# The order of the last routing steps, and who loads the last batch's second-layer weights

## What is computed

```python
xn = _layernorm(x)
x = x + gnn(xn, src, dst, edge_weight) + mix(xn)     # message passing; linear attention over 8 heads, gelu
h = _layernorm(x)
probs = softmax(h @ gate_w + gate_b)                 # 8 experts, top 1
idx = argmax(probs)
pos = (cumsum(one_hot(idx), axis=0) * one_hot(idx)).sum(-1) - 1
kept = pos < C                                       # C = ceil(1.25 * 12500 / 8)
hmid = relu(buf[e] @ w1[e] + b1[e])                  # 256 -> 1024
y = hmid @ w2[e] + b2[e]                             # 1024 -> 256
x = x + nan_to_num(y[idx, pos] * prob * kept)
```

## Time and profile before

| | |
|---|---|
| median of 3 runs | 2496.98 us (2493.55 to 2497.48) |
| the profiled execution | 2497.35 us, of which the profile's span is 2495.6 us |
| TensorE | 2049.6 us busy (82%) |
| weight loads of TensorE | 1578.1 us (63%) |
| VectorE | 1511.6 us (61%) |
| ScalarE | 1033.6 us (41%) |
| GpSimd | 1849.9 us (74%) |
| DMA | 568.84 MB, 228 GB/s in the mean |

### The profile page before, as it was taken

How to read it: one execution, slowest core, us unless ns; L and a number is a source line. 1 busy time by engine, 2 the same in 40 slices (tenths; PEclk the granted TensorE clock), 3 DMA queues, 4 the chain that set the end, 5 groups by cost and what they waited for, 6 DMA issues and landing times. The chain is left out here.

```text
span 2495.6 us, 42607 instructions
## 1 busy us (share of the span) xinstructions
PE 2049.6 (82%) x12873; PEld 1578.1 (63%) x12873; DVE 1511.6 (61%) x5293; ACT 1033.6 (41%) x2479; POOL 1849.9 (74%) x1924
## 2 busy tenths in 40 slices
PE   0048999994677787998989989998989998787997
PEld 0015666662455565776768777776778777676986
DVE  6776555554358777787747556566565666565332
ACT  4663333331244444543434433443444444352332
POOL 7777777777777777777777777777777777765575
PEclk9999999996788887999999999999998999898999
DMA  9846666664566667777777777777887888778653
GB/s 337 321 138 178 174 175 175 175 172 128 150 195 201 194 190 255 237 238 222 244 232 227 248 231 234 233 229 253 304 295 273 306 304 293 249 274 305 239 180 108
DMA packets 279195, 568.84 MB, mean 228 GB/s; under 512 B 51493, under 2 KB 180142, under 8 KB 259791
## 3 DMA queue, kind: packets, MB, share of 16 engines
q0 software_dynamic: 98352, 268.90, 35.3%
q1 hardware_dynamic: 150225, 245.97, 28.9%
q10 hardware_dynamic: 30390, 51.21, 5.6%
HBM read 506.09 MB, written 87.86 MB: 238 GB/s over the span
## 5 line engine op out<-in xcount | busy, mean ns | idle before, releaser
L967 POOL DMA_INDIRECT rows_sb<-xn_scratch,src_sb x1517 | 1458.3, 961 | 462.2 <-issue 456.7
L1261 PE MATMUL bank<-acc 128*128 128x128 f32 (+1 forms) x2624 | 434.4, 319 | 3.6 <-ACT acc L2042 2.9
L1285 PE MATMUL bank<-acc 128*128 128x256 f32 x1680 | 413.1, 390 | 0.0
L1261 PEld LDWEIGHTS bank<-acc 128*128 128x128 f32 x2624 | 379.2, 202 | 27.3 <-issue 5.6
L1079 PE MATMUL bank<-rows_sb,s_sb 128*24 128x256 f32 x3082 | 229.7, 419 | 198.6 <-DMA rows_sb<-xn_scratch,src_sb 198.0
L2059 ACT ACTIVATE acc<-bank,acc 128x128 f32<-128x128 f32 (+1 forms) x656 | 211.9, 398 | 368.5 <-PE bank L1261 368.2
L1285 PEld LDWEIGHTS bank<-acc 128*128 128x128 f32 x1680 | 313.9, 194 | 48.8 <-issue 0.4
L1549 DVE TENSOR_TENSOR acc<-acc,bank 128x48 f32 x831 | 170.5, 205 | 264.8 <-PE bank L1089 150.2
L1079 PEld LDWEIGHTS bank<-rows_sb,s_sb 128*24 128x24 f32 x3082 | 85.5, 108 | 272.8 <-issue 240.4
L1976 ACT COPY sums<-bank 120x256 f32<-120x256 f32 x208 | 76.5, 368 | 355.6 <-PE bank L1079 355.5
L2007 ACT ACT_TABLE_LOAD x95 | 121.9, 1283 | 200.8 <-PE bank L1168 199.9
(11 more groups left out here) (277 smaller groups left out, 3633.7 us busy)
## 6 DMA issues: line engine op xcount, KB each, us to landing
acc<-ffn_first_in SPq DMA_DIRECT2D x64, 1028.0 KB
acc<-ffn_w_in SPq DMA_DIRECT2D x64, 1024.0 KB
arena<-xn_scratch SPq DMA_DIRECT2D x194, 128.0 KB, 3.1
h_scratch<-arena ACTq DMA_DIRECT2D x97, 256.0 KB
rows_sb<-xn_scratch,src_sb POOLq DMA_INDIRECT x1517
xnt_scratch<-arena SPq DMA_DIRECT2D x97, 128.0 KB, 2.3
arena<-xnt_scratch SPq DMA_DIRECT2D x97, 128.0 KB
arena<-x_in SPq DMA_DIRECT2D x97, 128.0 KB
```

The lines of the kernel that those rows point to most:

```text
L967: pool.indirect_dma_start(out=chunk_row(c), out_offset=None, in_=xn_d, in_offset=bass.IndirectOffsetOnAxis(ap=src_sb[:, c:c + 1], axis=0)) ...
L1261: m = pe.matmul(bank[:, i * tokens:(i + 1) * tokens], w1_sb[k % 2][:, h, f * P:(f + 1) * P], xt[:, k % 2, h, 0:tokens], start=h == 0, stop ...
L1285: m = pe.matmul(bank[:, i * D:(i + 1) * D], hid[:, f, i * P:(i + 1) * P], w2_sb[k % 2][:, f, :], start=False, stop=f == FC - 1 and i == 0)
```

## The change

Two edits, both for the last batch.

First, the order at places 215 to 220. On TensorE, tick 162, first(58, a), moves from ahead of "sums" to behind it. On VectorE, the spread for that tick stays ahead of the routing work (called by hand under "early"), the rank is read after the fourth of the seven tables, not after the seventh, and the two `finish_unit` steps of units 56 and 57 (places 215 and 216) move to the end of place 217, behind `fill_slots`. On GpSimd, the scatters of units 56 and 57 move from places 216 and 217 to place 218, behind the gathers of units 60 and 61. The wanted place of units of the last batch is one higher, so that the turn of unit 60 moves from place 219 (ahead, before first(59, b)) to place 220, behind second(59, a).

Second, the second-layer weights of units 64 to 81 are loaded by SyncE's `load_second`, for each of the 18 units, also where the expert is the one of unit k - 2. The 18 indirect DMAs of GpSimd fall away, the first-layer weights stay with GpSimd. The places (`w2_at`) stay: place 227 for unit 64, and every second one from there.

```diff
@@
-        new1_ld, new2_ld, rows_known = sems("new_w1_ld", 2), sems("new_w2_ld", 2), sem("rows_known")
+        new1_ld, rows_known = sems("new_w1_ld", 2), sem("rows_known")
@@
         sums_at = [p + 1 for p in chosen_at]
+        HELD = range(chosen_at[-1], last_c + 1)
+        assert HELD[0] > PAIRS and rank_at[-1] == sums_at[-1] == build_at[-1]
...
-        wanted_at = [slots_at[b] + (4 if slots_at[b] + 4 < PAIRS else 2) for b in batch_of]
+        wanted_at = [slots_at[b] + (4 if slots_at[b] + 4 < PAIRS else 2 if slots_at[b] < PAIRS else 3) for b in batch_of]
...
-            if e_place[n] == sums_at[-1] and ("unit", n - 1) not in here:
-                here.insert(0, ("unit", n))
-            elif e_place[n] >= PAIRS or ("unit", n - 1) in here or after == len(here):
+            if e_place[n] >= PAIRS or ("unit", n - 1) in here or after == len(here):
                 here.append(("unit", n))
...
-            asked = max(known - 1 + lag, turn_place[k] - ahead)
+            asked = max(known - 1 + lag if slots_at[batch_of[k]] < PAIRS else known, turn_place[k] - ahead)
...
-            scatter_at[min(done_place(k) + 1, PLACES - 1)].append(k)
+            scatter_at[last_c + 1 if done_place(k) in HELD else min(done_place(k) + 1, PLACES - 1)].append(k)
@@ sync_program
                 for k in w2_at[p]:
-                    if k not in SKIPS:
-                        load_second(k)
+                    load_second(k)
@@ gpsimd_program
-                for k in w2_at[p]:
-                    if k in SKIPS:
-                        load_new_second(k)
@@ tensor_program, second_layer
-                    if k in SKIPS:
-                        pe.wait_ge(new2_ld[k % 2], new_value(k))
-                    else:
-                        pe.wait_ge(w2_ld[k % 2], w2_value(k))
+                    pe.wait_ge(w2_ld[k % 2], w2_value(k))
@@ vector_program, side_step
                 elif kind == "early":
                     for t, s in c_steps(k, (2,)):
                         c_step(t, s)
+                    if k == sums_at[-1]:
+                        for n, at in enumerate(e_place):
+                            if at == k:
+                                unit_tick(n)
                     read_small(k, False)
                 elif kind == "end":
-                    read_small(k, True)
+                    if k != rank_at[-1]:
+                        read_small(k, True)
...
                         if build_at[t] == k:
                             build_table(t)
+                            if t == routes[-1][RT - 1]:
+                                read_small(k, True)
                 elif kind == "unit":
-                    unit_tick(k)
+                    if e_place[k] != sums_at[-1]:
+                        unit_tick(k)
@@ vector_program, the loop over places
-                for kind, k in side[p]:
-                    if kind == "unit" and p >= PAIRS:
-                        finish_unit(k)
+                if p >= PAIRS and p not in HELD or p == last_c:
+                    for n, at in enumerate(e_place):
+                        if at == p or p == last_c and at in HELD:
+                            finish_unit(n)
```

More of the change, by code:

```diff
@@ L1020, in load_new_first @@
                     bounds_check=NE * P - 1, oob_is_err=False).then_inc(new1_ld[k % 2], 16)
[L1022 to L1028, removed]
             for p in range(PLACES):
```

## The result

The changed kernel takes 2512.15 us (median of 6 runs, 2507.35 to 2519.01) against 2497.68 us of the kernel before (6 runs, 2493.55 to 2499.53): ratio 1.0055, 95% interval 1.0042 to 1.0067. It is 13.7 us slower by the ratio, where 3.8 us were forecast, and it lies outside the range.

What follows compares the result with a forecast made beforehand. In the last 230 us it saw the routing chain, token fetch and GpSimd's queue as bounds. Routing -2.0, GpSimd relieved -2.8, SyncE's queue +8.6 gave +3.8 us upon 2496.98: 2500.8 us, range 2492 to 2506.

Steps and rivals of the forecast that it cites:

- What bounds the kernel, and the mechanism: Last 230 us: routing chain and token fetch, GpSimd's 7.95 us a unit; then second-layer weights waiting behind load_back on SyncE.
- The forecast 2.8 us: Tail: GpSimd, relieved of 18 DMAs, no longer drops behind, so 2.3 and 0.53 us come back; lower bound 1.5.
- Landing behind load 7: Unit 67: second-layer weights land late behind load 7's megabyte on SyncE; wait taken as 3.0 us, bounds 0 to 4.5.
- rival (b): Units 67, 71: GpSimd's megabyte shares evenly, wait 4.5 us each; 2504.7 us, chance 0.30 with far parts of two other rivals.
- The clock: TensorE in the tail: a wait of 3 us costs about 1.1 us more afterwards at 1.2 GHz, range 0.9 to 1.6.
- Unit 75: Second layer of unit 75: half a megabyte ahead and no new expert beside it, 0 to 1.3 us, say 0.4.
- SyncE's queue in sum: Units 67, 71 and 75: waits and slow clock together cost 4.1, 4.1 and 0.4, sum 8.6 us, bounds 0 to 12.
- The routing order: Places 215 to 220: the first edit starts first(60, a) near 2305.3, not 2307.45; gain 2.0 us, bounds 0.5 to 3.5.
- Rival (c): Routing: reordering brings nothing, VectorE's two finishes end an equally long idle time; 0 instead of -2.0, 2502.8 us; no separate chance.
- nothing in the change moves these two: Routing: load 4 and unit 58's weights behind it keep their issue times, so "rank" stays at 2282.66 to 2283.5.
- (a): Tail: no wait for second-layer weights, both megabytes land within 6.85 us of load 7's issue; -4.8, 2492.2 us, chance 0.18.
- (d): Tail: GpSimd was not the cause of the small waits; between 2495 and 2503.6 us; no separate chance.

Runs made afterwards that it cites:

- e7: Changed kernel with loads 7 to 9 two places later and behind the weights there, loads 0 to 6 left ahead: 2494.56 us, 0.9977.
- e5: Changed kernel with GpSimd's 18 first-layer loads of units 64 to 81 out of bounds, moving nothing: 2508.95 us, one execution.
- e2: Kernel before with only the second edit, SyncE loading the second-layer weights of units 64 to 81: 2515.23 us, 1.0062.
- e6: Changed kernel with loads 7 to 9 fetching 16 numbers a partition instead of 2048: 2490.45 us, one execution.
- e9: Kernel before with the second edit, load_back behind the weights at all places and loads 7 to 9 two places later: 2500.82 us, 0.9995.
- e10: Changed kernel with load_back behind the weights, loads 7 to 9 two places later, finishes of units 56 and 57 behind unit 59's spread: 2485.60 us, 0.9935.
- e12: The same kernel as e10 measured a second time, on another chip, against the kernel before: 2486.05 us, 0.9940.
- e3: Changed kernel with load_back issued behind the weights of its place instead of ahead of them: 2490.27 us, 0.9965.
- e4: As e3, with the finishes of units 56 and 57 also moved behind the spread for unit 59: 2487.55 us, 0.9951.
- e1: Kernel before with only the first edit, the routing order; GpSimd still loads the second-layer weights: 2499.33 us, 0.9996.
- e8: Kernel before with only load_back issued behind the weights at all places, neither edit: 2504.21 us, 1.0010.
- e11: As e4 but with the second edit undone, loads 7 to 9 at their places: 2491.63 us, 0.9961.

## Why the prediction was wrong, point by point

**What bounds the kernel, and the mechanism: right.** The place (units 67, 71, 75), the order of SyncE's queue and its offsets came as worked out: load 7 at T + 2.99 (forecast 3.0), load 8 at T + 3.00, the weights at T + 4.28 (forecast 4.1). GpSimd has 1.4 us of idle time a unit and the 2.3 us of before are no longer lost; e7 shows a tail with no wait at all. The forecast 2.8 us came as 2.3 in the tail (2.1 in e7) and 0.6 behind the turn of unit 81, so this term held. What it did not have are the further 1.9 us between the last scatter and the end of the span.

**Landing behind load 7: mis-sized.** I had two rows: 9.1 us for a megabyte behind a megabyte, and 10.9 us for three megabytes at 327 GB/s, and took a wait of 3.0 us "nearer the lower row since it is the same queue and pattern". It is not the same pattern: in the row of 9.1 us GpSimd had no megabyte under way, and e5, where it moves none, took 9.0 us (2363.41, load 7's issue, to 2372.42). From load 7's issue to the products it took 11.2 us (2359.21 to 2370.44), close to the upper estimate, and the weights came at T + 14.2, where I had written T + 14 "or so". So the wait was 4.30 us, and 4.02 at unit 71, 2.3 us more in sum than forecast: nearly rival (b)'s 4.5, past its deciding point of T + 13.3. By the Trainium skill (DMA: Bandwidth & Descriptors, "Queues, rings and completion order") the weights stay behind load 7 in the ring and share round robin with GpSimd: the trace agrees with both halves, 7.7 us with load 7 alone and 9.9 us with both. The Trainium skill's fit (the same page, "Anatomy of one DMA — SWDGE (gpsimd) path") is for one DMA from GpSimd; carried over to SyncE's pair it gives an estimate of 6.8 us. The measured times are 9.0 us with other traffic beside the pair and 11.2 us with the third megabyte, so the estimate does not hold here.

**The clock: mis-sized.** I took 1.1 us (0.9 to 1.6) from one block of sixteen products after a 5.08 us wait. After the waits of 4.30, 4.02 and 3.39 us it was 3.09, 2.82 and 2.97 us, because the eight products behind the wait ran at 1.2 GHz to the end and most of the next sixteen too. The row used showed only one block of the slow stretch; its neighbour, the turn with 0.66 us and not 0.38, would have given more. At units 67 and 71 this is 3.7 us of the miss (3.09 + 2.82 - 2.2).

**Unit 75: wrong.** I gave it 0.4 us since load 9 is half as large and no new expert is beside it. It waited 3.39 us and lost 6.36. Load 9 did not go out at T + 3.0 but at T + 5.45 (2437.93 against the turn at 2432.48), since the scatters it waits for stood behind GpSimd's first-layer load of unit 75, and that went out 6.58 us after the turn of unit 74, not 4.25 us as those of units 65 to 73 did:

```profile
2426.69 0.98 POOL L997 DMA_INDIRECT out_dram<-acc,sca_i  x1 [0.30 <-issue]
2431.30 1.05 POOL L1016 DMA_INDIRECT acc<-ffn_first_in,acc  x1 [3.62 <-issue]
```

The same 6.58 us stand in the run without first-layer bytes, and the delay is at this unit in every profile read for it (after, e2, e5, e6, e7, e9, e10, e12; longer still in e3 and e4). The trace names no releaser, and the cause is open (a 16 KB transfer on an instruction queue begins within 0.8 us of that issue in nine profiles, before it in some and behind it in others, and no run tests it); before, GpSimd had no idle time there in which it could be seen. Unit 75 cost 6.0 us more than forecast, half of it wait and half clock: the forecast's step that failed is that load 9 leaves at T + 3, and 2.5 us of the wait are that.

**SyncE's queue in sum:** 8.6 us forecast with bounds 0 to 12, 20.6 us in the profile. The 12.0 us between them are the 2.3, 3.7 and 6.0 of the three points above, more than the whole miss in the profile (14.6 - 3.8 = 10.8): the routing gained 1.2 us less than forecast, against that stand the 1.9 us at the end, 0.4 ahead of the first mark and 0.1 of GpSimd's term. That these partly hide the error is luck. The bounds of the wait at units 67 and 71, 0 to 4.5 us, held; the upper bound of the sum did not, because it had the clock at 1.6 us at most and unit 75's wait at 1.3.

**The routing order: right in its steps, smaller in its gain.** "Sums" came at 2268.36, `find_full` was done at 2274.1 (forecast 2275.1), "rank" at 2282.49, not earlier, as forecast; the spread for unit 59 began at 2299.63 (2300.6), the wait for it was 3.72 us, the wait at unit 60's turn was gone. First(60, a) began at 2303.86, earlier than the forecast 2305.3 (before: 2307.45), but took 3.75 us at the lower clock and not 1.95, and the eight products behind it 2.46 and not 1.89, so that 0.8 us of the forecast 2.0 are left at unit 61: the clock again, which I had charged to second(59, a) alone; in time, the first edit alone lies between 3.7 us gained and 1.5 us lost (e1). Rival (c) is as good a description as the forecast. What I missed is that load 4 ahead of unit 58's weights was no fixed fact: the argument "nothing in the change moves these two" was true, but it named the lock and did not ask who held it. Turned round together with the new order it was worth more than either edit (e1, e8, e11).

**The rivals.** (a), no wait, is out. (b) named the mechanism and its deciding point rightly, and its 2504.7 us was short by the clock and unit 75. (d) is out: with the order mended the tail has no wait. The chance of 0.30 for slower than the forecast was too low: the 10.9 us, worked out from a row with the same three streams, should have weighed more than the 9.1 us from a row with two.

## What to carry to other kernels

When a load is moved to another queue, write down what stands ahead of it there and until when each of these waits: here 1 MB that was in no hurry, ahead of 1 MB that was needed in 9.85 us, cost more than all 18 issues on the relieved engine had. Put loads with a deadline ahead of those without, and move the others half a period away, where nothing follows for some us (e7: 6.9 us to the next). And size a wait by the row that has all streams of the new situation, with the clock that follows it counted over every block until it is back. To place a gain, cut the timeline at marks that the edit can't move: the first one used here moved with `load_back`, and made 3 us of routing gain between e11 and e12 where there were 0.6.

## What the runs showed of the hardware

- After a wait in the tail the slower clock costs time beyond the wait: 2.8 to 3.1 us after 3.4 to 4.3 us in the changed kernel, 1.7 to 2.6 us after 3.9 to 4.8 us in e2, 1.7 us after 1.77 us in e1 and after 2.09 us in e5; but 0.04 us after 1.25, 1.78 and 2.23 us in e3 and e4 and after 1.47 us in e5. The wait's length alone does not tell it.
- With the tail at 247 GB/s and not 197, GpSimd's small scatters of unit rows took 6.1 us to land (median), against 2.4 before, and in e7 at 279 GB/s 6.0; no wait on TensorE is put down to them.
- An indirect DMA whose row numbers all lie out of bounds costs GpSimd's queue as much as any other, 1.05 us and 0.3 us of gap (e5, unit 76's first-layer load at 2433.27); only its bytes are saved.
- The routing of the same code, from the earlier mark, took 49.4 to 52.8 us in four profiles (after, e5, e6, e7), and 54.1 and 56.1 us in two others (e8, e9), by waits and by the clock's level: there a difference of 3 us between two profiles says nothing. With the new order, `load_back` behind and the finishes moved it took 42.2 to 42.8 us in four (e4, e10, e11, e12).
- From the last scatter to the end of the span it is 9.1 us where GpSimd has the 18 indirect loads of second-layer weights and 7.2 us where it has not, in 14 profiles without exception.
